# A transformer block on one core: where two pairs of score-maximum units stand in the opening of the program

## What is computed

```
x = layernorm(x + attention(x))      # layer norm before Q, K, V inside; causal softmax; Wo, bo
x = layernorm(x + ffn(x))            # a mixture of 8 low-rank maps, weighed by a softmax of a small MLP

Q, K, V = split_heads(Xn @ Wq + bq), split_heads(Xn @ Wk + bk), split_heads(Xn @ Wv + bv)
scores = Q @ K^T / sqrt(16), masked above the diagonal
A = softmax(scores); AV = A @ V; return AV @ Wo + bo
```

## Time and profile before

| | |
|---|---|
| median of 3 runs | 431.72 us (431.71 to 434.21) |
| profiled execution | 431.88 us |
| its span | 429.9 us |
| TensorE busy | 405.0 us (94%) |
| VectorE busy | 307.0 us (71%) |
| ScalarE busy | 243.3 us (57%) |
| GpSimd busy | 78.5 us (18%) |
| DMA, mean | 49 GB/s |
| mean granted TensorE clock | 0.996 |

### The profile page before, as it was taken

How to read it: one execution, slowest core, us unless ns; L and a number is a source line. 1 busy time by engine, 2 the same in 40 slices (tenths; PEclk the granted TensorE clock), 3 DMA queues, 4 the chain that set the end, 5 groups by cost and what they waited for, 6 DMA issues and landing times.

```text
span 429.9 us, 7414 instructions
## 1 busy us (share of the span) xinstructions
PE 405.0 (94%) x2565; PEld 213.7 (50%) x2565; DVE 307.0 (71%) x807; ACT 243.3 (57%) x541; POOL 78.5 (18%) x115
## 2 busy tenths in 40 slices
PE   7997899999999989999999999999999998999994
PEld 3545444344334444476668734344334444446783
DVE  5548997798798676438488799789889863213665
ACT  6646555666777576443451264667676847642421
POOL 4422211143250110102240022113212011020000
PEclk9999999999999999999999999999999999999998
DMA  6167860450402000002673045054130000000011
GB/s 196 23 97 101 196 97 10 74 76 8 72 19 82 2 2 0 2 1 74 106 130 59 26 79 91 7 84 70 20 57 3 0 3 1 2 0 2 0 50 49
DMA packets 18452, 21.14 MB, mean 49 GB/s; under 512 B 4976, under 2 KB 11888, under 8 KB 18416
## 3 DMA queue, kind: packets, MB, share of 16 engines
q1 hardware_dynamic: 18365, 20.66, 25.7%
q10 hardware_dynamic: 51, 0.01, 0.0%
HBM read 5.79 MB, written 2.10 MB: 18 GB/s over the span
## 4 chain that ended last, share of the span: by engine, by line
PE 76%; DVE 15%; ACT 6%; issue 2%; DMA 1%; POOL 0%; ACTq 0%; DVEq 0%; POOLq 0%
PE ps L953 19%; PE ps L1068 14%; PE ps L1047 14%; PE ps L1024 10%; DVE mx L824 8%; PE ps L961 8%; PE ps L969 4%; PE ps L944 2%; ACT pr L683 2%; PE ps L1028 2%; PE ps L1142 2%; PE ps L1078 1%; DVE ps L820 1%; ACT stk L604 1%; DMA stq<-mrow 1%
## 5 line engine op out<-in xcount | busy, mean ns | idle before, releaser
L683 ACT ACTIVATE pr<-ps 128x512 f32<-128x512 f32 (+3 forms) x384 | 165.9, 495 | 95.3 <-PE ps L1047 93.8
L824 DVE TENSOR_REDUCE mx<-ps 128x1 f32<-128x512 f32 (+3 forms) x240 | 145.7, 665 | 14.6 <-PE ps L1024 7.4
L1047 PE MATMUL ps<-stq,stk 99*128 99x512 bf16 (+3 forms) x384 | 116.2, 330 | 4.8 <-ACT pr L683 3.3
L1024 PE MATMUL ps<-stk,stq 96*128 96x512 bf16 (+3 forms) x384 | 112.5, 327 | 1.4 <-DVE mx L824 0.6
L595 POOL TENSOR_SCALAR_AFFINE_SELECT pr<-pr 128x512 f32<-128x512 f32 x64 | 40.9, 639 | 245.9 <-ACT pr L683 245.9
L1068 PE MATMUL ps<-pr,va 128*32 128x512 f32 (+3 forms) x768 | 81.8, 498 | 0.0
L1047 PEld LDWEIGHTS ps<-stq,stk 99*128 99x128 bf16 x384 | 34.4, 98 | 90.8 <-ACT pr L683 51.8
L1024 PEld LDWEIGHTS ps<-stk,stq 96*128 96x128 bf16 x384 | 37.5, 98 | 21.4 <-issue 5.6
L820 DVE CUSTOM_DVE_ANT_0 ps<-ps,causal 128x384 f32<-128x384 f32 (+1 forms) x64 | 38.5, 648 | 11.6 <-PE ps L1024 11.6
L1028 PE MATMUL ps<-mask,ident_b 128*128 128x128 bf16 x192 | 35.2, 219 | 0.0
L953 PE MATMUL ps<-u_t,avt 128*128 128x256 f32 x128 | 30.8, 383 | 0.3 <-ACT avt L719 0.2
(11 more groups left out here) (108 smaller groups left out, 389.1 us busy)
## 6 DMA issues: line engine op xcount, KB each, us to landing
stq<-qk_raw SPq DMA_DIRECT2D x32, 96.0 KB, 2.8
stk<-qk_raw SPq DMA_DIRECT2D x32, 96.0 KB, 2.8
x_in<-in_x SPq DMA_DIRECT2D x8, 256.0 KB, 3.5
stq<-qk_raw SPq DMA_DIRECT2D x32, 64.0 KB, 2.4
stk<-qk_raw SPq DMA_DIRECT2D x32, 64.0 KB, 2.4
out_y<-x SPq DMA_DIRECT2D x3, 512.0 KB, 3.1
stk<-qk_raw SPq DMA_DIRECT2D x32, 32.0 KB, 2.4
stq<-qk_raw SPq DMA_DIRECT2D x32, 32.0 KB, 2.1
```

The lines of the kernel that those rows point to most:

```text
L683: nc.scalar.activation(probs(b, g, s)[:, j, q0 - c * CHUNK:], act_bank(ev)[:, q0 - c * CHUNK:], ACT.Exp, scale=DH ** -0.5).then_inc(s_act_ ...
L824: nc.vector.tensor_reduce(dst, src, AX.X, ALU.max).then_inc(s_dve_free, 1)
L1024: last = nc.tensor.matmul(bank[:, i * w:(i + 1) * w], q[0:ROWS, t // TPC, j, tile(t % TPC)], k[0:ROWS, k0 // CHUNK, j, 0:w], start=True, s ...
L1047: nc.tensor.matmul(bank[:, q0 - c * CHUNK:], stk[stack_of(b, g)][0:ROWS + PARTS, kt // TPC, j, tile(kt % TPC)], stq[stack_of(b, g)][0:ROWS ...
```

## The change

Four projections of chunk 1, in the order Q0, K0, Q1, K1 (the digit is the half of the features), are mixed with the units of the first two heads. Before, `woven` put them as Q0, K0, unit 1, Q1, units 3, 4, 7, K1, unit 8. Now the order is written out: Q0, K0, units 1 and 3, Q1, unit 4, K1, units 7 and 8. The second edit takes the first two units of the second block (0 and 1) ahead of the last value projection and of the rows event; before, the projection and the rows stood ahead of all units of the second block. Nothing is added to or removed from the computation. Sequence 1 is not touched.

```diff
         if b == 0:
             at_split = opening.index(("split", 0, 0, 0))
             near = sum(ev[0] == "max" and max_units(tiles)[ev[3]][3][-1] < HPG // 2 for ev in opening[:at_split])
-            order += qks[:2] + woven(qks[2:-1], opening[:near]) + qks[-1:]
-            order += woven(opening[near:at_split], vs[0][2:3]) + [opening[at_split]] + vs[0][3:] + opening[at_split + 1:]
+            order += qks[:2] + opening[:2] + qks[2:3] + opening[2:3] + qks[3:] + opening[3:near]
+            rows, *rest_of_opening = opening[at_split + 1:]
+            order += woven(opening[near:at_split], vs[0][2:3]) + [opening[at_split]] + rest_of_opening[:2] + vs[0][3:] + [rows] + rest_of_opening[2:]
```

## The result

Over 19 executions of each on the same chips the changed kernel takes 433.49 us (432.5 to 435.35) and the kernel before 431.77 (431.55 to 434.21). The ratio is 1.0041 with a 95% interval of 1.0033 to 1.005: slower, by 1.7 us, which is 0.4% of the time. The forecast was 433.2. The profiled execution took 433.99, 2.1 over the profiled one of before, and that difference has two parts, of which the forecast held only one.

A forecast was written before the change was run, and what follows sets the result against it. It took the first score's start at 41.67 as the pivot whose shift reaches the end in full. Profiled 431.88 plus 1.47, the first edit's 1.0 already lost inside, gave 433.35; the median, 0.16 lower, 433.2; range 431.3 to 434.9.

The forecast's parts named there:

- Edit one: Projections among the first units: fourth projection and VectorE's split start sooner, worth -1.0, bounded by 0 and -1.3.
- Edit two: Two units ahead of last value projection wait for head group 1's load: +1.47 with the first edit's gain lost inside.
- VectorE's second idle stretch: VectorE waits from near 41.9 until 43.78 for the unit behind the first score, idle 1.9.
- the small DMA of the row maxima: DMA from ScalarE's queue that the first score waits for; took 3.10 before, with what follows the drain assumed to shift rigidly.
- That everything behind the score shifts with it: Past the first score, VectorE's unbroken row then TensorE's program pass the score's gain or loss to the end in full.
- Rival 1, the clock: TensorE's clock also falls after idle gaps around the last value projection, starving VectorE: +1.6, giving 434.8; chance 0.19.
- The 2.4 us read at the end of the trace: Time without a matmul at the trace's end, taken as enough for the clock to fall to 1.2 GHz.
- Rival 2, the backlog: From 38 to 63.84 VectorE's total work counts, not the first score's start: about 1.0 faster, 430.7; chance 0.06.
- Rival 3: The second block's units find their operands ready at 34.6, so the score starts 0.2 sooner: 431.5; chance 0.08.

The follow-up runs named there:

- The two kernels without the wait: Changed kernel with the last value projection ahead of the two units, 431.86; changed kernel with the second block's units sorted, first two heads first, 432.06.
- the kernel with one unit behind the projection: First edit alone with the second block sorted, plus one of its units between last value projection and rows: 431.45, ratio 0.9986.

## Why the prediction was right, and where its size was not

**Edit one** held in each step: the fourth projection at 27.83 (27.7 forecast), the split at 36.22 (36.0), and by itself -0.94 in the medians and -1.07 at the first score (-1.0).

**Edit two** held in its mechanism for the late score: the unit starts at 36.44 (36.33), the value projection at 37.24 (37.14), the drain at 39.22 (39.12), VectorE's second idle stretch is there (1.70; 1.9). The two kernels without the wait show that the load made most of the late score. One term of the sum was off: the small DMA of the row maxima took 2.65 in this execution and 3.10 in the one of before, so the score came at 42.79 instead of 43.14, +1.12 instead of +1.47. I had carried the 3.10 over as rigid; in the profiles of the other runs it is 2.55 to 3.03, so it is a term that varies from execution to execution.

**That everything behind the score shifts with it** held to a tenth wherever the clock stayed up: 1.07 at the score and 1.09 at the turn of the chain for the first edit alone, and 22.15 to 22.21 from the score to the turn in all eleven such profiles. In the changed kernel it did not hold between these two points: +1.12 became +2.18, by the clock. Behind the turn it held again, +2.18 there and 2.2 in the span.

**Rival 1, the clock,** was given 0.19 and was there in 22 of 31 executions of the changed kernel, as far as the mean clock tells; its price was given as 1.6 and measured as 1.06 in the profile and 0.8 to 1.1 in the lists. So it was partly luck that the forecast of 433.2 came close to the median of 433.49; two errors went against each other: the late score is cheaper than forecast (433.0 and 432.7 without a fall), and the fall, left to a rival, is in most executions. The step that failed is the weighing of that rival, "the gap here is split by 4 us of work, which speaks against". The work between the two gaps did not keep the clock up. The 2.4 us read at the end of the trace was no measure either: at the ends of the other traces the clock fell 2.1 to 4.6 us behind the last matmul. And kernels whose one profile shows a gap of 1.33 or 1.96, without a fall in that execution, have a fall in half of their others. What decides it in one execution stays open: the kernel before, with 1.39 in its profile, has a fall in 18 of 103.

**Rival 2, the backlog,** is out by the second edit alone and by the kernel with one unit behind the projection: VectorE's earlier start is given back ahead of the unit behind the score. **Rival 3** is out by the 1.48 of waiting.

## What to carry to other kernels

Work that is moved forward to fill one engine's idle time brings its operands' waits with it; before moving it, look up when its last load lands, not only whether its engine is free, and ask what is queued behind it on its own engine. Giving the faster consumer its work earlier can lengthen the feeding engine's gap ahead of the next real wait, and on TensorE such a gap can have a price of its own (0.4 to 1.1 us here, in some executions and not in others). When the times of a kernel fall into heaps, sort them by the granted clock before explaining the median.

## What the runs showed of the hardware

- The clock does not fall in every execution of the same kernel, by the mark of the mean clock. The gap ahead of the score in the kernel's profile and the executions with a fall: 2.32 and 2.43, 22 of 31; 2.36, one of 5; 2.30, 8 of 12; 2.05, 9 of 12; 1.96, 6 of 12; 1.39 (before), 18 of 103; 1.33, 6 of 12; 1.03, one of 11; 0.62 and 0.87, none of 24. The gap's length in one profile does not say whether it falls. 4 to 11 matmuls without use in the gap take it from half or more of the executions to one of 28.
- In the three profiles with a fall the clock fell 0.3, 0.7 and 1.5 us after the matmuls had started again, not in the gap itself, and in these three it cost less the later it fell (1.06, 0.9, 0.4).
- The wait for the same twelve DMAs ended at 35.86, 36.29, 36.44 and 37.24 in executions of kernels that differ little. Of these 1.4 us about 0.7 was already there when the first of SyncE's loads was issued (17.77, 17.70, 17.86 and 18.47), and most of the rest is one DMA whose issue took 0.96 to 1.63, while its neighbours took 0.59. An order that waits for the load inherits that spread.
